# A decoder in one kernel: where the trials of a weight quantiser run during self attention

## The chip, the cores and the metric

The kernel runs on one core of a Trainium2 chip. The time is device time in microseconds from the start to the end of one execution, the median of several runs. The core has five engines with a queue of their own each, which meet only through semaphores: TensorE (PE in the profile) for matmuls, VectorE (DVE), ScalarE (ACT), GpSimd (POOL), and SyncE (SP), which here only issues DMAs.

## What is computed

The program is a decoder of two layers over x (16 batches of 100 rows of 512): a first layer with latent attention, cross attention and a feed-forward part of signs, and a second layer with causal self attention (16 heads of 128), attention over a memory and a feed-forward part. The weights of that last part go through a quantiser before they are used, and it is this quantiser that the change is about. Cut to what matters, the reference does this for each block of 64 weights:

```python
amax = jnp.max(jnp.abs(wb), axis=-1, keepdims=True)
base = jnp.maximum(amax, 1e-08) / QMAX                       # QMAX = 15
for s in SHRINKS:                                            # 16 values, 0.4 to 1.0
    scale = base * jnp.asarray(s, dtype=w.dtype)
    deq = jnp.clip(jnp.round(wb / scale), -QMAX, QMAX) * scale
    err = jnp.sum((deq - wb) ** 2, axis=-1, keepdims=True)
    upd = err < best_err
    best_err, best_scale = jnp.where(upd, err, best_err), jnp.where(upd, scale, best_scale)
deq = jnp.clip(jnp.round(wb / best_scale), -QMAX, QMAX) * best_scale
```

There are two such weights of 2048 x 512. Nothing needs the result before the last phase, so the quantiser is laid beside the work of earlier phases, a chunk of 128 x 512 weights at a time.

## The kernel before

Nine phases follow each other: latent attention (three phases), the projection of k and v for cross attention, cross attention, the first feed-forward part, self attention (`mha`, tiles named `mh_...`), the attention over the memory (`me_...`), and the last feed-forward part (`fq_...`). For each phase each engine has its instructions in an order written out by hand. The first weight is quantised beside three phases before self attention; self attention quantises the whole second weight, 16 chunks (`NC = 16`).

Self attention runs over 64 pairs of a head and a group, here called slots (4 passes of 4 heads over 4 groups of 4 batches). In slot n, TensorE computes the scores of slot n, the projections q and k of slot n+1, some of v, the attention of slot n-1, and parts of the output projection; ScalarE copies out of PSUM and takes the exponentials; VectorE masks, takes maxima and makes the `lo` halves (every matmul is done with weights split in a `hi` and a `lo` half, three matmuls for one). In certain slots (n modulo 16 in 12 to 15, 0, 1, 3, 4) two weight pieces are turned by TensorE as well. From slot 55 on a tail is added in each slot: a row block is turned back, added and normalised, and GpSimd computes its reciprocal root (L2670, L2672). Nine tails fall in slots up to 63, seven into the slots behind them.

Each slot has four steps of the quantiser, so a chunk takes four slots and has 16 trials, one for each step. For a chunk i, with k the step counted from its start:

- steps 0 and 1, VectorE, `before`: the block maxima, the base and `a`, the absolute weights in units of the base (L1042 to L1052);
- the trials. On GpSimd, `pool_trial`: four instructions that each need the one before (L1085, L1087, L1089, L1091). They scale `a`, round it by adding and subtracting a large number, clip it, scale it back and subtract it from `a`. GpSimd has no other order than one trial after the other. On VectorE, `dve_unit`: two instructions at step s+2 (L1075 into a tile of `uint8`, which rounds; L1077, the difference);
- step s+3, ScalarE, `square`: the square of the error, in place (L1166);
- step s+4, VectorE, `sum_up`: the sum over each block of 64 (L1069);
- steps 20 to 23, VectorE, `after`: the least error, the scale that belongs to it and the quantised weights (L1143 to L1159).

The errors lie in a ring of three tiles (`mh_quant_d`). So trial u, on either engine, waits until trial u-3 is summed up:

```python
def error_free(self, eng, i, s):
    if self.mixed:
        u = 16 * i + s - 3
        if u >= 0:
            eng.wait_ge(self.summed.sem, self.summed.done(u // 16, u % 16))
```

Which trials run on VectorE is one tuple, `QUANT_ON_DVE`, that only self attention hands to its quantiser. It is read where the engines' programs place the trials:

```python
if 0 <= k - 2 < 16 and k - 2 in qz.on_dve:       # do_dve, quant(at)
    qz.dve_unit(i, k - 2)
...
if i < NC and s not in qz.on_dve:                # do_pool
    qz.pool_trial(i, s)
```

`square` waits for the semaphore of the engine that made the error, and the semaphores' counts are taken from the same tuple.

Of the kernel before, what the change touches and what calls it, by code (L numbers as in the profile page):

```python
# [52 lines left out]
ROW = V_AT + DH  # L53

QMAX = 15
QUANT_ON_DVE = (3, 8, 13)
QBLK = 64
SHRINKS = [float(np.float32(s)) for s in np.linspace(0.4, 1.0, 16)]
QCOLS = 512
# [47 lines left out]
def decoder(nc, t, out, stages=6):  # L107
# [2040 lines left out]
    def mha():  # L2148
# [30 lines left out]
        NC = 16  # L2179
        qz = Quantiser(ph, ctx, t["L1_ffn_w_proj"], w_proj_q, 0, NC, on_pool=True, depth=2, on_dve=QUANT_ON_DVE)  # L2180
        item_banks, score_bank, turn_bank, z_bank, y_bank, aux_bank = bank[0:3], bank[3], bank[4], bank[5], bank[6], bank[7]
# [798 lines left out]
```

## Time and profile before

| | us |
|---|---|
| median of 3 runs (3586.99 to 3593.51) | 3590.18 |
| the profiled execution, its own time | 3588.55 |
| its span, from the first to the last instruction | 3586.7 |
| PE, DVE, ACT, POOL busy in it | 2995.5, 2219.3, 1670.7, 1309.7 |
| granted clock of TensorE, mean over the span | 0.878 of full speed |

The profile is one execution. Busy times are sums over the span; an engine that shows 84% is not the limit in every phase, so the phases are read one by one. A line Lnnn is a line of the kernel, and where a helper issues the instructions of many tiles the tile's name tells them apart.

### The profile page before, as it was taken

How to read it: one execution, taken by the hardware profiler on the slowest of the kernel's cores; microseconds unless marked ns; L12 is line 12 of the kernel's file. 1: busy time of each engine (PE TensorE's matmuls, PEld its weight loads, DVE VectorE, ACT ScalarE, POOL GpSimd, SP SyncE). 2: the span in 40 equal slices, each digit the busy share in tenths (PEclk: the TensorE clock that was granted, in tenths of full speed). 3: DMA queues.
4: the chain of work that ended last, by engine and by line, in shares of the span. 5: the costliest groups of instructions: out<-in, count | busy, mean ns of one | idle time of the engine just before them, and what ended most of it. 6: DMA issues, size and time to landing. Idle time of an engine off the chain costs nothing. (4 is left out here: it accounts for less than half of the span.)

```text
span 3586.7 us, 50463 instructions
## 1 busy us (share of the span) xinstructions
PE 2995.5 (84%) x16144; PEld 2651.1 (74%) x16144; DVE 2219.3 (62%) x4458; ACT 1670.7 (47%) x4231; POOL 1309.7 (37%) x1609
## 2 busy tenths in 40 slices
PE   5799999986599999997687689999999965658988
PEld 4588877765588888885576678888888854548888
DVE  3333377774487888886367647777676776763333
ACT  1144444441388878774343355566565533332121
POOL 0000023220177666764000047788788860000000
PEclk9755599996799999998799889999999976779999
DMA  4432234443433333322311132212212113332000
GB/s 135 156 73 70 70 122 145 140 136 103 144 123 117 114 106 105 112 86 80 115 34 33 54 108 70 76 62 73 73 40 68 45 55 110 101 103 63 27 27 27
DMA packets 217223, 313.96 MB, mean 88 GB/s; under 512 B 47554, under 2 KB 113190, under 8 KB 214918
## 3 DMA queue, kind: packets, MB, share of 16 engines
q1 hardware_dynamic: 217030, 311.57, 28.0%
q8 instruction: 99, 1.62, 0.2%
q14 instruction: 94, 0.77, 0.1%
HBM read 215.15 MB, written 96.37 MB: 87 GB/s over the span
## 5 line engine op out<-in xcount | busy, mean ns | idle before, releaser
L1400 POOL TENSOR_TENSOR kv_krs<-kv_kms,minus_half 128x4 f32<-128x4 f32 x48 | 49.1, 1023 | 691.4 <-DVE kv_kms L1390 691.4
L1091 POOL TENSOR_TENSOR mh_quant_d<-mh_quant_a,mh_quant_d 128x512 f32<-128x512 f32 x208 | 277.5, 1334 | 17.3
L1166 ACT ACTIVATE mh_quant_d<-mh_quant_d 128x512 f32<-128x512 f32 x256 | 159.8, 624 | 111.0 <-POOL mh_quant_d L1091 110.7
L1069 DVE TENSOR_REDUCE mh_quant_err<-mh_quant_d 128x8 f32<-128x512 f32 x256 | 173.4, 678 | 37.4 <-ACT mh_quant_d L1166 35.7
L1668 PE MATMUL bank<-ga_eT,ga_v 128*128 128x400 f32 (+1 forms) x384 | 169.7, 524 | 29.6 <-DVE ga_zl L1854 29.3
L1085 POOL TENSOR_SCALAR mh_quant_d<-mh_quant_a 128x512 f32<-128x512 f32 x208 | 132.8, 638 | 133.8 <-DVE mh_quant_err L1069 86.1
L1625 PE MATMUL bank<-ga_xt,ga_wqh 128*128 128x400 f32 x512 | 177.7, 409 | 1.6 <-DVE ga_xt L162 1.6
L1818 ACT ACTIVATE ga_e<-ga_e,ga_nm 100x361 f32<-100x361 f32 x256 | 152.8, 597 | 38.9 <-DVE ga_nm L1913 37.2
L1124 POOL TENSOR_TENSOR ga_quant_d<-ga_quant_a,ga_quant_near 128x512 f32<-128x512 f32 x128 | 165.2, 1291 | 13.4 <-DVE ga_quant_err L1069 2.9
L1814 ACT ACTIVATE ga_e<-ga_e,ga_rs 100x361 f32<-100x361 f32 x256 | 152.7, 596 | 18.1 <-DVE ga_rs L1895 18.1
L1907 DVE SCALAR_TENSOR_TENSOR ga_e<-bank,ga_qrs,ga_mask 100x361 f32<-100x361 f32 x256 | 151.1, 590 | 13.9 <-PE bank L168 12.8
L2123 DVE TENSOR_TENSOR fq_v<-fq_v 128x400 f32<-128x400 f32 x64 | 36.8, 576 | 198.2 <-ACT fq_v L2096 198.2
L1089 POOL TENSOR_SCALAR mh_quant_d<-mh_quant_d 128x512 f32<-128x512 f32 x208 | 137.8, 662 | 17.2
L1797 ACT ACTIVATE ga_eT<-bank 128x300 f32<-128x300 f32 x256 | 106.2, 415 | 78.5 <-PE bank L1658 77.4
L1913 DVE TENSOR_REDUCE ga_nm<-ga_e 100x1 f32<-100x361 f32 x256 | 135.4, 529 | 6.7
L1087 POOL TENSOR_SCALAR mh_quant_d<-mh_quant_d 128x512 f32<-128x512 f32 x208 | 133.1, 640 | 17.2
L525 POOL TENSOR_TENSOR fq_var<-fq_mv,eps_ln 100x4 f32<-100x4 f32 x4 | 0.8, 198 | 375.7 <-DVE fq_mv L508 375.7
L2523 ACT ACTIVATE mh_e<-mh_e,mh_nm 100x100 f32<-100x100 f32 x256 | 93.7, 367 | 90.2 <-DVE mh_nm L2638 90.2
L2096 ACT ACTIVATE fq_v<-bank 128x400 f32<-128x400 f32 x64 | 32.3, 504 | 211.2 <-PE bank L168 211.2
L1941 POOL TENSOR_TENSOR ga_qrs<-ga_qms,minus_half 100x4 f32<-100x4 f32 x64 | 68.0, 1063 | 165.7 <-DVE ga_qms L1848 165.7
L525 POOL TENSOR_TENSOR fs_var<-fs_mv,eps_ln 100x4 f32<-100x4 f32 x4 | 0.8, 200 | 334.7 <-DVE fs_mv L508 334.7
L861 ACT ACTIVATE m_e<-bank,m_nm 128x128 f32<-128x128 f32 x200 | 70.7, 365 | 104.1 <-DVE m_nm L884 104.1
(429 smaller groups left out, 10655.4 us busy)
## 6 DMA issues: line engine op xcount, KB each, us to landing
keys_turned<-kv_kt SPq DMA_DIRECT2D x16, 1448.0 KB, 6.1
ga_kt<-keys_turned SPq DMA_DIRECT2D x64, 362.0 KB, 3.0
ga_xt<-x_turned SPq DMA_DIRECT2D x48, 400.0 KB, 5.0
mh_xt<-x_turned SPq DMA_DIRECT2D x48, 400.0 KB, 4.5
qkv<-m_rows SPq DMA_DIRECT2D x16, 1000.0 KB
m_rows<-qkv SPq DMA_DIRECT2D x50, 320.0 KB, 3.0
kv_ctx<-in_ctx SPq DMA_DIRECT2D x32, 256.0 KB, 6.4
values<-kv_v SPq DMA_DIRECT2D x16, 512.0 KB, 3.0
```

What stands on the lines that cost most here:

```text
L1069: nc.vector.tensor_reduce(self.of(self.err, i)[:, s, :], self.error(i, s), AX, ALU.add).then_inc(self.summed.sem, 1)
L1087: nc.gpsimd.tensor_scalar(e, e, MAGIC + QMAX, MAGIC, ALU.min, ALU.max).then_inc(made.sem, 1)
L1089: nc.gpsimd.tensor_scalar(e, e, -MAGIC, SHRINKS[s], ALU.add, ALU.mult).then_inc(made.sem, 1)
L1091: nc.gpsimd.tensor_tensor(e, a[:], e, ALU.subtract).then_inc(self.diff.sem, 1)
L1124: nc.gpsimd.tensor_tensor(self.d[s % 2][:], a[:], near[:], ALU.subtract).then_inc(self.diff.sem, 1)
L1166: nc.scalar.activation(self.error(i, s), self.error(i, s), ACT.Square).then_inc(self.squared.sem, 1)
L1625: last = nc.tensor.matmul(ps, wq[c // 2][:, k, w_], xt[:, k, c % 2, :], start=n == 0, stop=n == 11, skip_group_check=True)
L1668: last = nc.tensor.matmul(z_bank[:, 0:N], v[m % 3][0:kk, c, :], eT[m % 2][0:kk, c, :], start=c == 0, stop=c == 2, skip_group_check=True)
L1814: nc.scalar.activation(E[o % 4][:, 0:S2], E[o % 4][:, 0:S2], ACT.Copy, scale=rs[o % 4][:])\
L1818: nc.scalar.activation(E[n % 4][:, 0:S2], E[n % 4][:, 0:S2], ACT.Exp, bias=nm[n % 4][:], accum_out=sm[n % 4][:]).then_inc(exped.sem, 1)
L1907: nc.vector.scalar_tensor_tensor(out=E[n % 4][:, 0:S2], in0=score_bank[n % 2][0:S, 0:S2], scalar=qrs[g % 2][:, hh, j:j + 1], in1=small["ma ...
L1913: nc.vector.tensor_reduce(nm[n % 4][:], E[n % 4][:, 0:S2], AX, ALU.max, negate=True).then_inc(maxed.sem, 1)
```

## The change

All 16 trials of a chunk are made on GpSimd in self attention, and none on VectorE. Trials 3, 8 and 13 of each chunk were on VectorE. The tuple is the whole diff:

```diff
@@ -53,7 +53,7 @@
 QMAX = 15
-QUANT_ON_DVE = (3, 8, 13)
+QUANT_ON_DVE = ()
 QBLK = 64
```

With an empty tuple `dve_unit` is never called, `pool_trial` is called for every trial, and every square waits for GpSimd. The quantiser keeps its ring of three error tiles (it depends on the tuple being given, not on what is in it), and the other phases' quantisers don't read it.

## Rows read from the trace of the kernel before

**Rows 1.** The page: busy tenths in forty slices, TensorE and GpSimd

```profile
PE   5799999986599999997687689999999965658988
...
POOL 0000023220177666764000047788788860000000
```

**Rows 2.** Table of stretches: all trials, a light chunk, a heavy chunk

```profile
core 0: us, PE busy (x) PEld busy (x) DVE busy (x) ACT busy (x) POOL busy (x), PEclk, DMA share, GB/s
2094.70:2929.00 834.30, 762.38 (x4537) 696.85 (x4535) 593.60 (x1039) 482.16 (x1394) 687.38 (x850) 0.96 0.19 62
2413.65:2461.74 48.09, 44.21 (x268) 40.90 (x266) 34.34 (x62) 28.53 (x85) 42.96 (x53) 1.00 0.14 46
2512.56:2566.24 53.68, 50.90 (x298) 46.24 (x297) 36.49 (x66) 31.64 (x90) 42.62 (x54) 0.94 0.23 71
```

**Rows 3.** Waits of GpSimd and ScalarE: us in total, times, longest

```profile
POOL mh_quant_d L1085 <- DVE mh_quant_err L1069: 86.1, 44, 5.8
POOL mh_quant_d L1085 <- DVE mh_quant_a L1052: 40.0, 2, 39.3
...
ACT mh_quant_d L1166 <- POOL mh_quant_d L1091: 110.7, 72, 3.8
```

**Rows 4.** Groups of lines, VectorE: busy us, mean ns, idle us before

```profile
L1077 DVE SCALAR_TENSOR_TENSOR mh_quant_d<-mh_quant_r,mh_quant_a 128x512 f32<-128x512 uint8 x48 | 53.5, 1115 | 1.6
...
L1075 DVE TENSOR_SCALAR mh_quant_r<-mh_quant_a 128x512 uint8<-128x512 f32 x48 | 30.7, 640 | 0.7 <-DVE mh_quant_rscale L1151 0.2
```

**Rows 5.** Groups of lines, GpSimd, in the stretch of the trials

```profile
L1091 POOL TENSOR_TENSOR mh_quant_d<-mh_quant_a,mh_quant_d 128x512 f32<-128x512 f32 x208 | 277.5, 1334 | 17.3
L1089 POOL TENSOR_SCALAR mh_quant_d<-mh_quant_d 128x512 f32<-128x512 f32 x208 | 137.8, 662 | 17.2
L1087 POOL TENSOR_SCALAR mh_quant_d<-mh_quant_d 128x512 f32<-128x512 f32 x208 | 133.1, 640 | 17.2
L1085 POOL TENSOR_SCALAR mh_quant_d<-mh_quant_a 128x512 f32<-128x512 f32 x208 | 132.8, 638 | 133.8 <-DVE mh_quant_err L1069 86.1 <-DVE mh_quant_a L1052 40.0
L2672 POOL TENSOR_TENSOR mh_rstd<-mh_var,minus_half 100x1 f32<-100x1 f32 x9 | 5.6, 626 | 0.7
L2670 POOL TENSOR_TENSOR mh_var<-mh_mv,eps_ln 100x1 f32<-100x1 f32 x9 | 3.7, 407 | 0.0
```

**Rows 6.** Timeline of GpSimd: start us, duration us; starts of trials

```profile
2094.70 0.62 POOL L1085 TENSOR_SCALAR mh_quant_d<-mh_quant_a 128x512 f32<-128x512 f32 x1 [39.32 <-DVE mh_quant_a L1052]
...
2098.05 0.62 POOL L1085 TENSOR_SCALAR mh_quant_d<-mh_quant_a 128x512 f32<-128x512 f32 x1
...
2442.72 0.62 POOL L1085 TENSOR_SCALAR mh_quant_d<-mh_quant_a 128x512 f32<-128x512 f32 x1
...
2444.82 1.29 POOL L1091 TENSOR_TENSOR mh_quant_d<-mh_quant_a,mh_quant_d 128x512 f32<-128x512 f32 x1
2446.19 0.62 POOL L1085 TENSOR_SCALAR mh_quant_d<-mh_quant_a 128x512 f32<-128x512 f32 x1
...
2454.41 0.62 POOL L1085 TENSOR_SCALAR mh_quant_d<-mh_quant_a 128x512 f32<-128x512 f32 x1 [1.31 <-DVE mh_quant_err L1069]
```

**Rows 7.** Timeline of a slot with weight pieces: TensorE, GpSimd, VectorE

```profile
2507.05 0.39 PE L168 MATMUL bank<-mh_wvh,mh_xt 128*100 128x512 f32 x1
...
2515.54 1.12 PE L2338 MATMUL bank<-ident,raw 128*128 128x128 f32 x4 [2.55 <-DVE mh_wql L162]
...
2516.88 0.63 PE L167 MATMUL bank<-mh_wvl,mh_xt 128*100 128x512 f32 x1
...
2528.65 0.62 POOL L1085 TENSOR_SCALAR mh_quant_d<-mh_quant_a 128x512 f32<-128x512 f32 x1 [5.69 <-DVE mh_quant_err L1069]
...
2524.48 0.69 DVE L1069 TENSOR_REDUCE mh_quant_err<-mh_quant_d 128x8 f32<-128x512 f32 x1
```

**Rows 8.** Timeline: an instruction of GpSimd and one of VectorE side by side

```profile
2411.05 0.94 POOL L1089 TENSOR_SCALAR mh_quant_d<-mh_quant_d 128x512 f32<-128x512 f32 x1
...
2411.55 0.98 DVE L1052 TENSOR_TENSOR mh_quant_a<-mh_quant_a,mh_quant_rbase 128x512 f32<-128x512 f32 x1
```

## The prediction

> **What bounds the kernel now.** I read the page's forty slices first [rows 1]. They show nine phases in a row, and GpSimd (POOL) at six to eight tenths in slices 23 to 31 while TensorE (PE) stands at eight or nine tenths: that is the self attention with the quantiser of the change in it. Then the table of stretches [rows 2]: from GpSimd's first trial at 2094.70 to its last instruction of the trials at 2929.00 lie 834.3 us, PE busy in 762.4 of them, GpSimd in 687.4, VectorE (DVE) in 593.6, ScalarE (ACT) in 482.2. No single engine is full, so the waits must say who is late. They run in a ring [rows 3]: ACT waited 110.7 us, 72 times, for the last GpSimd instruction of a trial; GpSimd waited 86.1 us, 44 times, for DVE's sums before it could start one; PE was idle for 834.3 - 762.4 = 71.9 us. PE and GpSimd are thus both near their limit: GpSimd's idle time inside the stretch is 86.1 + 0.7 us (of the 40.0 us that it waited for L1052, 39.3 lie before the first trial [rows 3, 6]). That 86.8 us is all the cover that there is for more work on GpSimd. The question is whether 48 more trials fit into it.
>
> **The change, part by part.** Of 16 trials of a chunk, 3 run on DVE, in 16 chunks: 48 trials leave DVE and go to GpSimd, which then runs 256 instead of 208. The output is the same; the buffer of `uint8` stays allocated, so no tile moves. No DMA and no wait for a DMA changes.
>
> *Removed from DVE.* 48 L1075 at 640 ns and 48 L1077 at 1115 ns: 30.7 + 53.5 = 84.2 us [rows 4]. DVE is busy 593.6 of 834.3 us and would be at 61% of the same stretch. I count this relief as nothing, since what the sums (L1069) and squares (L1166) wait for from now on is GpSimd. If the cover were gone, and DVE paced the stretch, all 84.2 us could be given back.
>
> *Added to GpSimd.* A trial is four dependent instructions, L1085, L1087, L1089, L1091, with a mean of 638 + 640 + 662 + 1334 = 3274 ns busy [rows 5]. Between them lie gaps of some 0.08 us (17.2 us over 208, from each of the rows). What it really costs is the pitch. I take it from the whole stretch: 834.3 us, less 86.8 us of waiting, less the nine reciprocal roots of the tail that fall in it (407 + 626 ns and two gaps, 1.1 us each, 9.9 us), is 737.6 us for 208 trials, 3.55 us each. Single pitches bound it: without any stretched instruction, 3.35 us (2094.70 to 2098.05) is among the shortest and 3.47 us (2442.72 to 2446.19) stands for the commoner kind [rows 6]. So 48 trials are 48 x 3.55 = 170 us against 86.8 us of idle time. They don't fit, and 83 us are left over even if GpSimd never waits again.
>
> *Who waits then.* ACT's queue has each square at a fixed place, three steps behind the trial. While ACT waits there, behind it stand the copies of q, k and v out of PSUM, the exponentials and the `hi` halves of the weights; DVE's `lo` halves stand behind those, and PE needs both. So once GpSimd is late all the time, the four engines move at its pace. A chunk is four slots. In a light one GpSimd already sets this pace: trial 0 starts at 2413.65 and that of the next chunk at 2461.74, 48.1 us for 13 trials with one wait of 1.31 us, so 3.60 us a trial, while the granted PE clock was 1.00 [rows 2, 6]. With 16 trials at 3.55 us each a chunk takes 56.7 us, and I found none in the trace that takes that long now: the chunk from 2512.56 on, with weight pieces, takes 53.7 us from its trial 0 to the next one's [rows 2].
>
> *Are GpSimd's waits really gone?* GpSimd may start trial u when the sum of trial u-3 is made (three error buffers). One of the longest waits, 5.69 us before trial 4 at 2528.65, stands in a slot in which PE stopped for 2.55 us and then ran at half its pace (0.63 us for a matmul that took 0.39 us before the stop; the granted clock is 0.93 over its chunk, against 1.00 over the light one) [rows 2, 7]. The absent trial 3 would lie in just this hole. It may start after the sum of trial 0, which begins at 2524.48 and ends at 2525.17, and would run to 2528.6, when trial 4 may start anyway: there the added trial costs nothing, but 2.2 us of waiting (2522.96 to 2525.2) would stay. Ten of the 16 waits before trial 4 are of 2.9 us or more, so up to 22 us of waiting could survive. I expect less, because GpSimd has no slack behind it any more: ACT may find a trial late by about one pitch more than today, and that lag swallows 2 us. I put 4 us on it. The 1.31 us before trial 14, in nearly every chunk [rows 6], is filled by trial 13.
>
> *Collisions at the memory port.* When DVE runs an instruction with two SBUF inputs beside GpSimd, both can stretch: beside DVE's L1052 a GpSimd instruction of 0.62 us took 0.94 us [rows 8]. An undisturbed trial is 3 x 0.62 us for the instructions of L1085 to L1089 and 1.29 us for L1091, 3.15 us [rows 6]; the mean of 3.274 us [rows 5] is 0.12 us above it, 26 us over 208 trials. The DVE instructions that remain (L1049, L1052, L1156, L1159) cause most of it; the 48 pairs that leave I put at 5 us, with bounds of nothing and 20.
>
> The Trainium skill says in "SBUF — State Buffer", section "Who interferes with whom", that a DVE instruction with two SBUF inputs contends with a GpSimd instruction that reads SBUF, and that the later of the two is blocked for the whole instruction. The row beside L1052 agrees, with 0.32 us. By that rule each of the 48 L1077, which reads two tiles of SBUF beside a GpSimd that is nearly always busy, would have stretched GpSimd at least once; 48 x 0.32 = 15 us would come back by that estimate instead of my 5, and the sum would be +72 us. I stay at 5 since the rule also lets GpSimd be the one that holds the port, and L1077's own mean of 1115 ns [rows 4] says that it was DVE that waited.
>
> **The sum.** 256 x 3.55 + 9.9 = 918 us against 834.3: +83 us (with the unrounded pitch). Less 5 us of collisions, plus 4 us of waits that survive: +82 us. The drain behind it (to 2966 us, a chain of DMA, PE, DVE and GpSimd over the last tails) and the other eight phases I leave as they are; PE's clock in the stretch may fall, but PE has then 762 of 916 us to do and isn't late. Profiled execution: 3588.55 + 82 = 3671 us. The median of the runs shown is 1.6 us above that execution, so 3672 us, 2.3% slower.
>
> **Rivals.**
> - *The waits stay, or PE's clock joins in* (+100 to +170 us). For it: GpSimd's 86.8 us of waiting come from sums that are late in the slots with weight pieces, and PE's halved matmuls show what a hole of 2.55 us costs; a slower GpSimd makes more holes. If the 22 us of the heavy slots stay, +100 us; if every wait of today stays, 48 x 3.55 = +170 us, 3690 to 3760. Against it: the hole before trial 4 is where the moved trial goes. A halved clock in every slot's second half (some 2.5 us each) would bring PE's 47.6 us a chunk (762.4/16) to 57.6, just above GpSimd's 56.7.
> - *A trial gets cheaper on a GpSimd that never waits* (+30 to +65 us). If all pitches fell to 3.35 us, 256 x 3.35 + 9.9 = 868 us, +33 us, 3623; with the stretch of 0.12 us left on them +64 us. For it: the short pitch exists, and DVE's pairs no longer collide. Against it: short and long clean pitches follow the trial's number, not the load.
> - *DVE was the pace, and its relief pays for it* (not slower). GpSimd waited 86.1 us for DVE, and much of PE's idle time is a wait for DVE, as the 2.55 us are [rows 7]. For the time to stay the pitch would have to be (834.3 - 9.9)/256 = 3.22 us or less, which is under the 3.35 us of the short pitch [rows 6]. It decides only if GpSimd's instructions run in less than the shortest time that this trace has, and I see no reason for it; it would give 3590 us or, with DVE's relief on the path, some 3570.
> - *The change does nothing*: excluded, since the tuple is what places each trial on its engine.
>
> **Chances.** The forecast (GpSimd back to back, +65 to +100 us) 0.70; waits or clock 0.18, trials cheaper 0.09, not slower 0.03. Range: 3648 us (between the cheap trials and the forecast) to 3705 us (the 22 us of waits, some of the clock on top); about one case in ten is left out on either side. Likeliest case alone: 3655 to 3690. A measurement tells 0.2% from nothing here, 7 us; faster 0.01, same 0.02, slower 0.97.
>
> **What the profile after would show.** L1085 to L1091 256 times, L1075 and L1077 gone. GpSimd's stretch 900 to 935 us long and busy for over 90% of it; its waits for L1069 below 25 us in sum. ACT's wait for L1091 far above 110.7 us. PE's waits in the stretch doubled, its granted clock there at or below 0.96. Chunks of an even 56 to 58 us, light or heavy. If instead the waits for L1069 stay near 86 us, the first rival holds; if the pitch in the stretch is near 3.35 us, the second.

## The result and the profile after

The changed kernel takes 3678.9 us (median of 4 runs, 3674.5 to 3686.2) against 3590.75 us before (4 runs): 1.0248 times the time, 95% interval 1.0227 to 1.0269, or 88 us more (82 to 97 us). 3672 us was forecast, with a range of 3648 to 3705 us.

The profiled execution took 3682.08 us, 93.5 us above that of before, and its span is 3680.3 us. The page of the changed kernel, engines and two lines of the forty slices:

```profile
PE 3027.7 (82%) x16144; PEld 2676.4 (73%) x16144; DVE 2140.1 (58%) x4362; ACT 1673.0 (45%) x4231; POOL 1455.9 (40%) x1801
...
PE   5799898976699999985788689898988864658988
...
POOL 0000023320366666661000188999999970000000
```

Against [rows 1] GpSimd now stands at eight or nine tenths in slices 24 to 32 (counted from 1), where it stood at four to eight. (The six to eight tenths that the prediction read in slices 23 to 31 stand in slices 25 to 33.) Its table of stretches, for the trials (first trial to the last instruction of the tail that follows them), a light chunk and a chunk with weight pieces; columns as in [rows 2]:

```profile
core 0: us, PE busy (x) PEld busy (x) DVE busy (x) ACT busy (x) POOL busy (x), PEclk, DMA share, GB/s
2099.70:3020.10 920.40, 794.93 (x4537) 721.45 (x4535) 514.03 (x943) 484.17 (x1395) 832.89 (x1042) 0.92 0.18 56
2444.60:2501.20 56.60, 46.06 (x253) 42.45 (x252) 29.41 (x55) 28.96 (x85) 51.87 (x65) 0.92 0.12 40
2557.50:2613.90 56.40, 51.02 (x296) 46.38 (x294) 31.68 (x59) 30.66 (x89) 51.67 (x65) 0.94 0.21 67
```

The stretch of the trials went from 834.3 to 920.4 us. GpSimd is busy for 832.9 of them, 90%, and was for 82%. TensorE issues the same 4537 matmuls, but is busy for 32.6 us more with them (794.9 against 762.4): its granted clock is 0.92, where it was 0.96. VectorE has lost its 84 us of pairs and is busy for 79.6 us less (514.0 against 593.6), since some of its other instructions take longer now (L1157 1126 ns in the mean and not 703). A light chunk takes 56.6 us and one with weight pieces 56.4 us, where [rows 2] have 48.1 and 53.7. From one chunk's trial 0 to the next one's lie 56.3 to 60.6 us, in 13 of the 15 cases at most 58.3; before it was 48.1 to 56.0 us. The different chunks have become alike: that is what one engine's pace looks like. Waits in the stretch, GpSimd's and then ScalarE's:

```profile
POOL mh_quant_d L1085 <- DVE mh_quant_a L1052: 42.2, 2, 41.6
POOL mh_quant_d L1085 <- DVE mh_quant_err L1069: 10.9, 9, 2.5
...
ACT mh_quant_d L1166 <- POOL mh_quant_d L1091: 278.4, 161, 3.8
```

Of the first row 41.6 us lie before the first trial, so GpSimd waits 0.6 + 10.9 = 11.5 us in the whole stretch, where it waited 86.8 us. ScalarE waits 278.4 us for the last instruction of a trial, where it waited 110.7 us [rows 3]. The groups of GpSimd in the stretch:

```profile
L1091 POOL TENSOR_TENSOR mh_quant_d<-mh_quant_a,mh_quant_d 128x512 f32<-128x512 f32 x256 | 341.2, 1333 | 21.4
L1085 POOL TENSOR_SCALAR mh_quant_d<-mh_quant_a 128x512 f32<-128x512 f32 x256 | 165.0, 644 | 64.7 <-DVE mh_quant_a L1052 42.2 <-DVE mh_quant_err L1069 10.9
L1089 POOL TENSOR_SCALAR mh_quant_d<-mh_quant_d 128x512 f32<-128x512 f32 x256 | 164.1, 641 | 21.1
L1087 POOL TENSOR_SCALAR mh_quant_d<-mh_quant_d 128x512 f32<-128x512 f32 x256 | 159.8, 624 | 21.1
L2672 POOL TENSOR_TENSOR mh_rstd<-mh_var,minus_half 100x1 f32<-100x1 f32 x9 | 5.0, 556 | 0.7
L2670 POOL TENSOR_TENSOR mh_var<-mh_mv,eps_ln 100x1 f32<-100x1 f32 x9 | 1.7, 193 | 0.0
```

The mean of a trial is 644 + 624 + 641 + 1333 = 3242 ns, 32 ns less than in [rows 5]. Its pitch, worked out as in the prediction, is (920.4 - 11.5 - 9.9)/256 = 3.51 us, where it was 3.55. (The 9.9 us for the nine reciprocal roots are those of the kernel before; here the same instructions and their gaps take 7.4 us, with which the pitch is 3.52 us. The table below keeps to 9.9 us for all runs.) Of the 93.5 us between the two profiled executions the stretch explains 86; 5.0 us lie in front of it (the first trial starts at 2099.7 and not at 2094.7; in the experiments below it starts at 2099.8 to 2106.8, whatever they change) and some 2.5 us behind it.

Two chunks' first trials and a wait in the second of them, in the timeline of GpSimd, then the sum of VectorE that ends the wait:

```profile
2557.50 0.63 POOL L1085 TENSOR_SCALAR mh_quant_d<-mh_quant_a 128x512 f32<-128x512 f32 x1
...
2613.92 0.62 POOL L1085 TENSOR_SCALAR mh_quant_d<-mh_quant_a 128x512 f32<-128x512 f32 x1
...
2625.05 0.62 POOL L1085 TENSOR_SCALAR mh_quant_d<-mh_quant_a 128x512 f32<-128x512 f32 x1 [1.03 <-DVE mh_quant_err L1069]
...
2624.20 0.69 DVE L1069 TENSOR_REDUCE mh_quant_err<-mh_quant_d 128x8 f32<-128x512 f32 x1
```

From 2557.50 to 2613.92 a whole chunk of 16 trials passes in 56.4 us. It is the chunk of [rows 7], where GpSimd waited 5.69 us before trial 4; now it doesn't wait in this chunk at all. The wait of 1.03 us is that before trial 3 of the chunk behind it, which before waited 4.85 us before its trial 4.

### The profile page after: what moved, and what is told of

It reads as the page before. It is cut to its first block and busy times, and to the rows that moved or that the text cites. A ratio compares the mean times of both kernels' runs of the same rounds, so it can differ in the third digit from the quotient of the medians.

```text
span 3680.3 us, 50607 instructions
## 1 busy us (share of the span) xinstructions
PE 3027.7 (82%) x16144; PEld 2676.4 (73%) x16144; DVE 2140.1 (58%) x4362; ACT 1673.0 (45%) x4231; POOL 1455.9 (40%) x1801
## 5 line engine op out<-in xcount | busy, mean ns | idle before, releaser
L1091 POOL TENSOR_TENSOR mh_quant_d<-mh_quant_a,mh_quant_d 128x512 f32<-128x512 f32 x256 | 341.2, 1333 | 21.4
L1166 ACT ACTIVATE mh_quant_d<-mh_quant_d 128x512 f32<-128x512 f32 x256 | 160.7, 628 | 278.5 <-POOL mh_quant_d L1091 278.4
L1085 POOL TENSOR_SCALAR mh_quant_d<-mh_quant_a 128x512 f32<-128x512 f32 x256 | 165.0, 644 | 64.7 <-DVE mh_quant_a L1052 42.2
L1089 POOL TENSOR_SCALAR mh_quant_d<-mh_quant_d 128x512 f32<-128x512 f32 x256 | 164.1, 641 | 21.1
L1087 POOL TENSOR_SCALAR mh_quant_d<-mh_quant_d 128x512 f32<-128x512 f32 x256 | 159.8, 624 | 21.1
L1941 POOL TENSOR_TENSOR ga_qrs<-ga_qms,minus_half 100x4 f32<-100x4 f32 x64 | 68.1, 1065 | 166.2 <-DVE ga_qms L1848 166.2
L166 PE MATMUL bank<-mh_zh,mh_woh 128*128 128x400 f32 x256 | 97.6, 381 | 42.0 <-DVE mh_acc L2597 26.1
```

What stands on the lines that cost most here:

```text
L1085: nc.gpsimd.tensor_scalar(e, a[:], 1.0 / SHRINKS[s], MAGIC, ALU.mult, ALU.add).then_inc(made.sem, 1)
L1087: nc.gpsimd.tensor_scalar(e, e, MAGIC + QMAX, MAGIC, ALU.min, ALU.max).then_inc(made.sem, 1)
L1089: nc.gpsimd.tensor_scalar(e, e, -MAGIC, SHRINKS[s], ALU.add, ALU.mult).then_inc(made.sem, 1)
L1091: nc.gpsimd.tensor_tensor(e, a[:], e, ALU.subtract).then_inc(self.diff.sem, 1)
L1166: nc.scalar.activation(self.error(i, s), self.error(i, s), ACT.Square).then_inc(self.squared.sem, 1)
```

## The experiments

Each ratio is to runs of the kernel before on the same chip; "stretch" is that of the trials in the profiled execution, worked out like the two above, and "pitch" is the stretch less GpSimd's waits in it and 9.9 us for the tail, by the number of trials. The groups e1 to e4, e5 to e8 and e9 to e12 ran on a chip each, so ratios of different groups are compared with their intervals. In the cuts of code, waits for semaphores and their counts are left out.

| | GpSimd trials | ratio (95%) | stretch us | GpSimd waits us | pitch us |
|---|---|---|---|---|---|
| before | 208 | 1 | 834.3 | 86.8 | 3.55 |
| changed | 256 | 1.0248 (1.0227 to 1.0269) | 920.4 | 11.5 | 3.51 |
| e1, 8 on VectorE | 240 | 1.0105 (1.0077 to 1.0132) | 873.6 | 15.2 | 3.54 |
| e2, 3 and 11 on VectorE | 224 | 1.0088 (1.0061 to 1.0115) | 867.6 | 68.1 | 3.52 |
| e3, 1, 5, 9, 13 on VectorE | 192 | 1.0034 (1.0022 to 1.0046) | 851.3 | 160.7 | 3.55 |
| e4, uint8 trial | 256 | 1.125 (1.1222 to 1.1279) | 1284.0 | 0.0 | 4.98 |
| e5, four tiles | 256 | 1.0219 (1.0193 to 1.0246) | 909.5 | 2.2 | 3.51 |
| e6, four tiles, 3, 8, 13 | 208 | 1.0015 (1.0002 to 1.0028) | 836.3 | 92.8 | 3.53 |
| e7, pairs kept | 256 | 1.0254 (1.0234 to 1.0274) | 932.1 | 6.9 | 3.58 |
| e8, minimum and addition | 256 | 1.0575 (1.0552 to 1.0599) | 1041.5 | 0.0 | 4.03 |
| e9, no clip | 256 | 0.9967 (0.9950 to 0.9984) | 818.6 | 99.4 | 2.77 |
| e10, no clip, 3, 8, 13 | 208 | 0.9982 (0.9970 to 0.9993) | 828.3 | 241.7 | 2.77 |
| e11, first step on ScalarE | 256 | 1.0072 (1.0046 to 1.0098) | 852.6 | 139.0 | 2.75 |
| e12, the same, 3, 8, 13 | 208 | 1.0057 (1.0037 to 1.0078) | 849.0 | 262.9 | 2.77 |

### e1 to e3: how many trials on GpSimd

e1:

```diff
-QUANT_ON_DVE = ()
+QUANT_ON_DVE = (8,)
```

> Trial 8 of each chunk back on VectorE, the other 15 on GpSimd (240 trials). Theory (GpSimd's trials, back to back at 3.51 us, are the pace): 16 trials fewer on GpSimd take 56 us off the 920 us stretch, to about 866 to 875 us with a little more waiting; in all +30 to +45 us against the kernel before. Rival (it is the lost order of the work or TensorE's clock that costs): the time stays near that of the changed kernel, +70 us or more. Rival (VectorE's relief is worth something): less than 56 us comes back, since VectorE has 28 us more to do.

e2:

```diff
-QUANT_ON_DVE = ()
+QUANT_ON_DVE = (3, 11)
```

> Trials 3 and 11 of each chunk on VectorE, 14 on GpSimd (224 trials). Theory: GpSimd needs 224 x 3.51 + 10 = 796 us and some waiting, so the stretch falls to the 820 to 840 us that the other engines need, within 10 us of the kernel before. Rival (pace is GpSimd alone, without any other limit): 796 us, 38 us faster than before.

e3:

```diff
-QUANT_ON_DVE = ()
+QUANT_ON_DVE = (1, 5, 9, 13)
```

> Trials 1, 5, 9, 13 of each chunk on VectorE, 12 on GpSimd (192 trials). Theory: GpSimd is no longer near its limit (684 us), and VectorE gets 28 us more than before; the stretch is set by TensorE and the chains through ScalarE and VectorE, within 10 us of the kernel before on either side. Rival (GpSimd was the pace before too): 16 x 3.51 = 56 us faster than before.

The stretch of e1, in the table of stretches (length, then PE, PEld, DVE, ACT and POOL busy):

```profile
2104.80:2978.40 873.60, 776.38 (x4537) 708.69 (x4535) 545.68 (x975) 483.48 (x1395) 787.98 (x978) 0.94 0.19 59
```

16 trials fewer took 46.8 us off the stretch and the total stands at 1.0105, some 38 us above the kernel before, inside what was expected. The stretch gave back 46.8 us and not the full 16 x 3.51 = 56: the waits rose by 3.7 us, and the pitch by 0.02 us, some 5.7 us over 240 trials. That would fit the 16 pairs of VectorE that run beside GpSimd again, but no run shows it here. VectorE was busy for 32 us more in it than in the changed kernel (545.7 against 514.0) and the kernel got faster, so its relief was not what counted. Below 240 trials the time no longer follows their number. e2's stretch and GpSimd's waits:

```profile
2104.80:2972.40 867.60, 773.07 (x4537) 706.40 (x4535) 563.71 (x1007) 484.05 (x1395) 735.11 (x914) 0.95 0.19 60
```

```profile
POOL mh_quant_d L1085 <- DVE mh_quant_err L1069: 64.9, 28, 5.7
POOL mh_quant_d L1085 <- DVE mh_quant_a L1052: 45.8, 6, 42.6
```

The next 16 trials took 6.0 us off the stretch and not the 34 us or more that were expected, and the total of 1.0088 is 32 us above the kernel before, where at most 10 were expected: a miss. The pitch is hardly changed, 3.52 us; the time that GpSimd saved it now waits, mostly for the sums (64.9 us). The timelines show where. Trial 4 of the first chunk, in the kernel before and in e2:

```profile
2108.41 0.62 POOL L1085 TENSOR_SCALAR mh_quant_d<-mh_quant_a 128x512 f32<-128x512 f32 x1 [3.63 <-DVE mh_quant_err L1069]
...
2118.53 0.62 POOL L1085 TENSOR_SCALAR mh_quant_d<-mh_quant_a 128x512 f32<-128x512 f32 x1 [3.62 <-DVE mh_quant_err L1069]
```

Waits before trial 4 sum up to 51.3 us in the kernel before and to 46.0 us in e2, in 13 chunks each; in e1 and in the changed kernel, where GpSimd makes trial 3 itself, it waits nowhere before trial 4. So taking trial 3 off GpSimd mostly turned work into waiting. Held against the kernel before, e2 has 16 trials more on GpSimd, 56 us, but the waits fell by only 18.7 us, and the stretch grew by 33.3: idle time is cover only for work that lands in it. e3, with 16 trials fewer than the kernel before:

```profile
2106.80:2958.10 851.30, 766.61 (x4537) 703.30 (x4535) 613.25 (x1071) 482.00 (x1395) 635.92 (x786) 0.96 0.19 61
```

```profile
POOL mh_quant_d L1085 <- DVE mh_quant_err L1069: 158.8, 82, 4.4
POOL mh_quant_d L1085 <- DVE mh_quant_a L1052: 44.5, 4, 42.6
```

GpSimd is busy for 635.9 of 851.3 us and waits 160.7 us, and the kernel is slower than the one before, though by 0.3% only, some 12 us (10 were the bound). That denies that GpSimd's trials alone were the pace before the change. Why e3 is slower than (3, 8, 13) stays open: VectorE has more to do (613.3 us against 593.6) and its trials lie elsewhere, and no run keeps their number and moves only their places. GpSimd's waits are spread, 27 to 34 us each before trials 2, 3, 6, 10 and 14.

### e5 and e6: four error tiles

```diff
-self.d = [sb(n(f"d{k}"), wide, F32, ctx) for k in range(3 if self.mixed else 2)]
+self.d = [sb(n(f"d{k}"), wide, F32, ctx) for k in range(4 if self.mixed else 2)]
...
-return self.d[(16 * i + s) % 3 if self.mixed else s % 2][:]
+return self.d[(16 * i + s) % 4 if self.mixed else s % 2][:]
...
-u = 16 * i + s - 3
+u = 16 * i + s - 4
```

> The changed kernel (all trials on GpSimd) with four error tiles instead of three, so that trial u waits for the sum of trial u-4. Theory (GpSimd is busy without a break, its waits are 11.5 us in all): at most 12 us faster than the changed kernel, +76 to +90 us against the kernel before. Rival (the ring of three couples the engines and sets the pace of 3.51 us a trial): 25 us or more come back.

> The kernel before (trials 3, 8, 13 on VectorE) with four error tiles instead of three. Theory: the 86.8 us that GpSimd waits there are cover and partly on the path, since TensorE too is near its limit (71.9 us idle of 834.3); 5 to 20 us faster than the kernel before. Rival (GpSimd's waits lie in places where TensorE is the late one): no change.

e5's waits fell from 11.5 to 2.2 us and its stretch by 10.9 us; in time it is 1.0219 against 1.0248, some 79 us above the kernel before, as expected, with intervals that overlap. (One of its four runs took 12577 us at a mean granted clock of 0.211; it has no profile, why it did stays open, and the ratio is that of the other three, 3671 to 3679 us.) The ring of three thus costs some 10 us of the stretch after the change and does not set the pace. e6 gained nothing: 1.0015. I had expected it to be 5 to 20 us faster. With a fourth tile GpSimd waited 92.8 us instead of 86.8, less for the sums (62.9 us) and more for the next chunk's `a` (L1052). GpSimd's idle time in the kernel before is cover, as the prediction used it, but moving it by a fourth tile gained nothing.

### e7: the relief of VectorE taken away

The pairs run at their old places in VectorE's program. Their second instruction writes to a tile of its own, so they wait for each other and no longer for the ring:

```diff
-            nc.vector.scalar_tensor_tensor(out=self.error(i, s), in0=r[:], ...).then_inc(self.diff_dve.sem, 1)
+            nc.vector.scalar_tensor_tensor(out=self.aside[:], in0=r[:], ...).then_inc(self.rounded.sem, 1)
...
-                    if 0 <= k - 2 < 16 and k - 2 in qz.on_dve:
+                    if k - 2 in (3, 8, 13):
```

> The changed kernel, and VectorE still runs the 48 pairs of L1075 and L1077 of the kernel before at their places, the second into a tile that nobody reads (extra work; the output is the same). This takes only the relief of VectorE away. Theory (the relief is worth nothing but some collisions, put at 5 us with bounds of 0 and 20): 0 to 20 us slower than the changed kernel, +88 to +110 us against the kernel before. Rival (VectorE's relief of 84 us gave much back): 40 to 84 us slower than the changed kernel, +130 us or more.

The stretch, and the pairs' groups on VectorE:

```profile
2103.00:3035.10 932.10, 795.90 (x4537) 720.28 (x4535) 605.57 (x1039) 484.29 (x1395) 848.99 (x1042) 0.93 0.17 56
```

```profile
L1082 DVE SCALAR_TENSOR_TENSOR mh_quant_aside<-mh_quant_r,mh_quant_a 128x512 f32<-128x512 uint8 x48 | 60.5, 1260 | 1.6
...
L1080 DVE TENSOR_SCALAR mh_quant_r<-mh_quant_a 128x512 uint8<-128x512 f32 x48 | 33.4, 697 | 0.7 <-DVE mh_quant_rscale L1156 0.2
```

VectorE ran 605.6 us of work in the stretch, 91.5 us more than in the changed kernel, and the time is 1.0254 against 1.0248: no difference that the intervals allow to tell (2 us, give or take 10). In the profiled executions the stretch is 11.7 us longer; that of e7 was the slowest of its four runs, 6 us above their median. The pitch rose from 3.51 to 3.58 us, 16 us over 256 trials, and the waits fell by 4.6. GpSimd's own instructions got longer: it is busy for 849.0 us, 16.1 more. One of them beside a pair's second instruction, where the mean of its group is 1329 ns:

```profile
2115.46 0.98 DVE L1082 SCALAR_TENSOR_TENSOR mh_quant_aside<-mh_quant_r,mh_quant_a 128x512 f32<-128x512 uint8 x1
...
2115.99 1.58 POOL L1096 TENSOR_TENSOR mh_quant_d<-mh_quant_a,mh_quant_d 128x512 f32<-128x512 f32 x1
```

In the timelines 95 of GpSimd's instructions overlap one of the 48 L1082; in sum they run 20 us longer than the medians of their groups. So what the pairs cost is GpSimd's time beside them, some 16 us in these two executions. The rival, that 84 us of relief give much back, falls.

### e4, e8, e9: the length of a trial, with all trials on GpSimd

e4 rounds by writing a tile of uint8, e8 leaves the scaling back out, e9 leaves the clip out. e8 and e9 compute other errors and choose other scales; they are for the time alone:

```diff
 # e4
-            nc.gpsimd.tensor_scalar(e, a[:], 1.0 / SHRINKS[s], MAGIC, ALU.mult, ALU.add)
-            nc.gpsimd.tensor_scalar(e, e, MAGIC + QMAX, MAGIC, ALU.min, ALU.max)
-            nc.gpsimd.tensor_scalar(e, e, -MAGIC, SHRINKS[s], ALU.add, ALU.mult)
+            nc.gpsimd.tensor_scalar(r[:], a[:], 1.0 / SHRINKS[s], float(QMAX), ALU.mult, ALU.min)
+            nc.gpsimd.tensor_scalar(e, r[:], SHRINKS[s], None, ALU.mult)
 # e8
-            nc.gpsimd.tensor_scalar(e, e, MAGIC + QMAX, MAGIC, ALU.min, ALU.max)
-            nc.gpsimd.tensor_scalar(e, e, -MAGIC, SHRINKS[s], ALU.add, ALU.mult)
+            nc.gpsimd.tensor_scalar(e, e, MAGIC + QMAX, -MAGIC, ALU.min, ALU.add)
 # e9
-            nc.gpsimd.tensor_scalar(e, e, MAGIC + QMAX, MAGIC, ALU.min, ALU.max)
```

> All 16 trials on GpSimd as in the change, but each of three instructions: the first writes the scaled and clipped weight to a tile of uint8, which rounds it, the second scales it back, the third subtracts. Theory: the pitch of a trial falls by an instruction and its gap, 0.70 us, to 2.8 us; 256 of them are 717 us, less than the other engines need, and the time falls to that of the kernel before or below it, -35 to 0 us. Rival (the change costs by what waits on GpSimd's place in the chain, not by GpSimd's time): it stays 50 us or more above the kernel before. If the conversion to uint8 costs GpSimd extra, the pitch tells it.

> All trials on GpSimd, each of three float32 instructions: the instruction that scales the rounded weight back is left out (so the errors and the chosen scales are others), its predecessor clips and subtracts the large number at once. Theory (pace is the busy time of a GpSimd trial): the pitch falls from 3.51 to 2.81 us, 256 of them are 719 us, and the stretch is then set by TensorE and the chains at 780 to 830 us: 50 to 5 us faster than the kernel before. Rival (the place of the work, not its length, costs): +50 us or more against the kernel before.

> All trials on GpSimd, each of the three instructions of the changed kernel that take 0.62, 0.62 and 1.29 us there: the clip at 15 (L1087) is left out, so the errors and the chosen scales are others. e8, which was to shorten the trial, made it longer, because its instruction of minimum and addition took 1922 ns and not 614; this one uses only the pairs of operations that the kernel already has. Theory (pace is the busy time of the trial): pitch 3.51 - 0.70 = 2.81 us, 256 of them 719 us, so GpSimd is no longer the pace and the stretch is 790 to 840 us: 45 us faster to 5 us slower than the kernel before. Rival (the place of the work costs): +50 us or more.

e4 and e8 turned into their opposite: they made the trial longer. GpSimd's groups in e4, then in e8:

```profile
L1086 POOL TENSOR_SCALAR mh_quant_r<-mh_quant_a 128x512 uint8<-128x512 f32 x256 | 492.3, 1923 | 63.0 <-DVE mh_quant_a L1052 41.5
L1088 POOL TENSOR_SCALAR mh_quant_d<-mh_quant_r 128x512 f32<-128x512 uint8 x256 | 393.2, 1536 | 21.2
L1090 POOL TENSOR_TENSOR mh_quant_d<-mh_quant_a,mh_quant_d 128x512 f32<-128x512 f32 x256 | 327.3, 1279 | 21.3
```

```profile
L1087 POOL TENSOR_SCALAR mh_quant_d<-mh_quant_d 128x512 f32<-128x512 f32 x256 | 493.1, 1926 | 21.1
L1089 POOL TENSOR_TENSOR mh_quant_d<-mh_quant_a,mh_quant_d 128x512 f32<-128x512 f32 x256 | 329.6, 1288 | 21.3
L1085 POOL TENSOR_SCALAR mh_quant_d<-mh_quant_a 128x512 f32<-128x512 f32 x256 | 160.6, 627 | 53.5 <-DVE mh_quant_a L1052 41.4
```

An instruction of the same 128 x 512 elements takes 1923 and 1926 ns here, where all three of the changed kernel take 624 to 644 ns. Both expectations were wrong as to the price, and both runs still measure what they were for: at a pitch of 4.98 and 4.03 us GpSimd never waits inside the stretch (0.0 us), so the stretch is the sum of its trials, 1284 and 1042 us. The means of the instructions and some 0.08 us for each gap give the same pitch: 1923 + 1536 + 1279 ns and three gaps are 4.98 us. The other engines have the same work as in the changed kernel. e9 is the run in the other direction; its stretch and GpSimd's waits (41.9 us of the second row lie before the first trial):

```profile
2100.20:2918.80 818.60, 757.94 (x4537) 694.41 (x4535) 516.16 (x943) 481.60 (x1395) 665.68 (x786) 0.97 0.20 63
```

```profile
POOL mh_quant_d L1085 <- DVE mh_quant_err L1069: 84.6, 56, 3.9
POOL mh_quant_d L1085 <- DVE mh_quant_a L1052: 56.7, 14, 41.9
```

At a pitch of 2.77 us the same placing of the work, all 16 trials on GpSimd, is 12 us faster than the kernel before. GpSimd waits 99.4 us, TensorE is busy for 757.9 of 818.6 us at a granted clock of 0.97, and the added 88 us are gone, as expected. It was the length of the trials and not their place.

### e10 to e12: what GpSimd's room is worth

e10 is e9 with `QUANT_ON_DVE = (3, 8, 13)`. e11 moves the first of the four instructions to ScalarE and takes four error tiles; e12 is e11 with trials 3, 8, 13 on VectorE:

```diff
 # e11, in squares(at) of ScalarE's program
+            i, s = divmod(at - 1, 16)
+            if 0 <= i < NC and s not in qz.on_dve:
+                qz.first_of(i, s)
...
+        def first_of(self, i, s):
+            act.wait_ge(self.pre.sem, self.pre.at(i, "a"))
+            self.error_free(act, i, s)
+            nc.scalar.activation(self.error(i, s), self.of(self.a, i)[:], ACT.Identity, bias=magic[:, 0:1],
+                                 scale=1.0 / SHRINKS[s]).then_inc(self.first_made.sem, 1)
```

> The kernel before (3, 8, 13 on VectorE) with the clip left out of GpSimd's 13 trials of a chunk (the errors and the chosen scales are others). It shows what is left when GpSimd is far from its limit (208 x 2.81 = 585 us) while VectorE keeps its share. Theory: the stretch is what TensorE and the chains need, 790 to 835 us, and no shorter than that of e9, since GpSimd has room in both and VectorE has 84 us more here. Rival (GpSimd's trials were the pace of the kernel before too): 40 us or more faster than before.

> All trials off VectorE, and the first instruction of each (scale and add the large number) moved from GpSimd to ScalarE, one step behind its old place, with four error tiles. GpSimd's pitch is 2.81 us then, as in e9, and ScalarE gets 256 x 0.62 = 159 us more, 645 of some 830 us. Theory: GpSimd is not the pace, the time is near that of the kernel before, -30 to +30 us; if ScalarE's queue becomes the pace, up to +60 us. Rival (all trials off VectorE cost 88 us by their place): +80 us.

> As e11, but trials 3, 8 and 13 of a chunk stay on VectorE: ScalarE gets 208 x 0.62 = 129 us more, VectorE keeps its 84 us. Theory: a little slower than e11 or the same, because GpSimd has room in both and VectorE's pairs only add work: 0 to +20 us against e11. Rival (GpSimd is still short of time): faster than e11.

The stretch of e10, then that of e11 and GpSimd's wait there (43.2 us of it before the first trial):

```profile
2102.20:2930.50 828.30, 765.55 (x4537) 700.46 (x4535) 574.92 (x1039) 480.87 (x1395) 546.17 (x642) 0.96 0.19 63
```

```profile
2102.50:2955.10 852.60, 768.31 (x4527) 700.64 (x4525) 524.96 (x943) 629.96 (x1649) 669.35 (x786) 0.95 0.19 61
```

```profile
POOL mh_quant_d L1088 <- ACT mh_quant_d L1097: 182.2, 86, 43.2
```

e10 takes 0.9982 of the time before, against 0.9967 of e9; the intervals overlap, so whether VectorE's pairs cost anything once GpSimd has room (its stretch is 9.7 us longer) is not settled. It does say what the kernel before had to gain from GpSimd: with 208 trials at 2.77 us and 241.7 us of waiting the stretch is 828.3 us, 6 us less than at 3.55 us, and not the 40 us of the rival. e11 is 26 us slower than the kernel before and 62 us faster than the changed one, inside its wide forecast; GpSimd has room (139 us of waiting), and its waits now are for ScalarE, which carries 630.0 us. e12 is the same within the intervals, so whether it is the 0 to 20 us slower than e11 that were expected they can't tell. None of the versions that compute the reference beats (3, 8, 13).

## Why the prediction was right

- *GpSimd's trials become the pace.* Right, and shown: with all trials on GpSimd the time rises with the length of a trial (e4, e8) and falls with it, until GpSimd waits again (e9), and it follows the number of trials from 256 to 240 (e1). Below that it no longer does (e2, e3), as the prediction had it for the kernel before, where GpSimd was not the only one near its limit.
- *86.8 us of cover against 170 us of work.* Right. The cover was used up to 11.5 us. That it could be used so fully rests on where the moved trials land, as the prediction said of trial 3: in e2, which leaves trial 3 on VectorE, 68.1 us of waiting stayed.
- *3.55 us a trial, less 5 us for collisions.* The pitch is 3.51 us; 256 trials took 899 us where 903 were forecast. The term for collisions was somewhat small: the pitch fell by 0.034 us against the kernel before, 9 us over 256 trials (6 with each kernel's own time for the roots). The timelines of the kernel before agree: 47 of GpSimd's instructions overlap one of the 48 L1077, and in sum they run 8 us longer than the medians of their groups. My bounds of nothing and 20 us hold that. The reason given for the small term, that VectorE was the one that waited, holds in part: L1077 took 691 ns at the shortest and 1115 in the mean, but GpSimd's instructions got longer as well. The Trainium skill's rule in "SBUF — State Buffer", section "Who interferes with whom", had given an estimated 15 us. In the kernel before some of the pairs ran while GpSimd waited (the first L1077, at 2106.96, lies in the hole before 2108.41), so the 8 us lie between the two, nearer to 5; beside a GpSimd that hardly waits, in e7, it is 16 us.
- *4 us of waits that survive.* They were 11.5 us, 8.9 of them in the place that was named: before trial 3, for the sum of trial 0, in seven chunks (1.03 us at 2625.05). In the hole of [rows 7] itself, where the prediction's sum left 2.2 us, nothing was left. The 22 us did not come. (The prediction's granted clock of 0.93 for the chunk of that hole is 0.94 in [rows 2]; nothing hangs on it.)
- *The sum.* 256 x 3.51 + 9.9 + 11.5 = 920 us measured, 916 forecast. The pitch came out 4 us lower over 256 trials and the waits 7.5 us higher. The two misses offset each other in part, which is luck.
- *The other phases and the drain.* They were left as they are; 7 us of the profiled difference lie there, which one execution of each can't tell from their scatter.
- *TensorE's clock.* It fell from 0.96 to 0.92 in the stretch, and its matmuls took 32.6 us longer, without being the pace: the chunks' 56.4 us in which it is busy for 46 to 51 leave room for it. Its idle time went from 71.9 to 125.5 us, 1.7 times and not quite the doubling that was forecast.

## What to carry to other kernels

Add up an engine's pitch, not its busy time, over the stretch that it works in, and hold it against its waits in that stretch: the waits are the most cover that more work can have, and what doesn't fit is the price. Then look where the waits lie, since only work that lands in them is covered (e2). Taking 84 us of work off VectorE, which was not the late one, gave back nothing that the runs can tell from zero (e7), whatever its sum of busy time said. And price a replacement instruction on the engine that is to run it before counting instructions: here three were dearer than four.

## What the runs showed of the hardware

- On GpSimd the price of a two-operation instruction on 128 x 512 float32 depends on its pair of operations: multiply and add, minimum and maximum, add and multiply take 614 to 622 ns (medians); minimum and add took 1922 ns in e8, with the same tile in and out as minimum and maximum have.
- With uint8 it was dear as well: multiply and minimum from float32 to uint8 1923 ns, a lone multiply from uint8 to float32 1536 ns in the mean (e4). Whether the first is due to the pair or to the type these runs don't separate. VectorE did the first of these in 0.40 us at the shortest (L1075 of the kernel before at 2106.53, while GpSimd waited).
- 128 x 512 instructions of GpSimd stretch beside a VectorE instruction with two inputs in SBUF: 1.58 us beside L1082 where the median of the group is 1.29 (e7), and the 48 L1082 took 0.97 us at the shortest and 1.26 in the mean.
